# Two layers of graph attention and a routed MLP on one core: routing steps laid between the tiles' statistics

## The reference, cut to what matters

```
x = x + attention(layernorm(x), adj)     # masked softmax over the 64 nodes of a graph
x = x + moe(layernorm(x))                # 8 experts, the two with the largest probability

logits = x_norm @ Wr + br                # 8 per token
top two of softmax(logits)               # ties: the lower expert number first
layer 0: weights p1/(p1+p2), p2/(p1+p2);  layer 1: weights p1, p2
y = w1 * expert[i1](x) + w2 * expert[i2](x)
```

## Time and profile before

| | us |
|---|---|
| median of three runs | 943.96 |
| the three runs | 937.42, 943.96, 946.27 |
| profiled execution, its own time | 937.9 |
| its span | 936.0 |
| VectorE busy | 723.5 |
| block phase of layer 0, `x1w` starts of blocks 0 and 6 (36.53 and 159.01), 6 steps | 122.48 |
| block phase of layer 1, `x1w` starts of blocks 0 and 6 (492.55 and 630.68), 6 steps | 138.13 |

### The profile page before, as it was taken

The page is one execution under the profiler, slowest core; times in us unless marked ns, Lnnn a source line. Parts: engine busy times, 40 slices in busy tenths (PEclk is TensorE's granted clock), DMA queues, the critical chain, the costliest instruction groups (busy, mean ns, idle before and its releaser), DMA issues.

```text
span 936.0 us, 24539 instructions
## 1 busy us (share of the span) xinstructions
PE 711.8 (76%) x6599; PEld 563.6 (60%) x6600; DVE 723.5 (77%) x2663; ACT 491.9 (53%) x1113; POOL 546.9 (58%) x544
## 2 busy tenths in 40 slices
PE   3888877567999999999988887886277877777500
PEld 2666555363899999999556765765236765555400
DVE  6788889762799999999388899997517777787538
ACT  2455665410677777777136566565306655555234
POOL 0037777776277667767400567777764777777720
PEclk9977978857999999999999699798589999999855
DMA  8394333331233323324534454332333333333757
GB/s 228 94 189 116 106 99 95 96 106 61 70 91 87 87 81 85 87 81 136 165 112 125 137 145 150 91 91 74 99 92 100 100 105 99 96 102 99 240 226 321
DMA packets 129399, 111.47 MB, mean 119 GB/s; under 512 B 30306, under 2 KB 112681, under 8 KB 129352
## 3 DMA queue, kind: packets, MB, share of 16 engines
q1 hardware_dynamic: 112072, 77.04, 29.9%
q0 software_dynamic: 17280, 33.87, 11.0%
HBM read 60.32 MB, written 52.36 MB: 120 GB/s over the span
## 4 chain that ended last, share of the span: by engine, by line
PE 35%; DVE 25%; issue 19%; POOL 12%; DMA 5%; ACT 2%; SPq 1%; POOLq 1%; DVEq 0%; ACTq 0%
PE bank L631 10%; PE bank L645 10%; POOL row_buf L457 6%; POOL y_buf L465 6%; PE bank L520 3%; DVE xin L973 3%; DVE stat L912 3%; PE bank L569 2%; PE bank L617 2%; PE bank L517 2%; PE bank L501 2%; DVE x1w L1009 2%; DVE x1w L1013 2%; PE bank L687 1%; DMA xin<-x_buf 1%
## 5 line engine op out<-in xcount | busy, mean ns | idle before, releaser
L457 POOL DMA_INDIRECT row_buf<-pay,slot x256 | 253.4, 990 | 217.8 <-DVE slot L1079 139.7
L465 POOL DMA_INDIRECT y_buf<-g_y,g_dst x284 | 293.3, 1033 | 132.1 <-issue 87.1
L806 ACT ACTIVATE g_xT<-bank 128x512 f16<-128x512 f16 x142 | 84.7, 597 | 171.9 <-PE bank L617 169.0
L631 PE MATMUL bank<-g_xT,w 128*128 128x256 f16 x1278 | 165.8, 276 | 1.5 <-ACT g_xT L806 1.4
L569 PE MATMUL bank<-cst,tri 128*128 128x512 bf16 x518 | 120.2, 388 | 24.9 <-DVE w L1189 14.0
L631 PEld LDWEIGHTS bank<-g_xT,w 128*128 x1278 | 117.6, 99 | 18.6 <-issue 2.1
L569 PEld LDWEIGHTS bank<-cst,tri 128*128 128x128 bf16 x518 | 51.4, 100 | 83.9 <-issue 29.3
L645 PE MATMUL bank<-w,g_h 128*128 x1260 | 84.4, 219 | 17.7 <-DVE g_y L1234 17.7
L813 ACT ACTIVATE xn<-bank,b_cols 128x256 f32<-128x256 f32 x216 | 86.7, 474 | 20.2 <-PE bank L631 11.9
L813 ACT ACTIVATE xt<-bank,b_cols 128x256 f32<-128x256 f32 x210 | 84.4, 475 | 14.0 <-PE bank L631 10.7
L645 PEld LDWEIGHTS bank<-w,g_h 128*128 128x128 f16 x1260 | 76.1, 98 | 25.6 <-issue 23.1
(11 more groups left out here) (191 smaller groups left out, 1312.9 us busy)
## 6 DMA issues: line engine op xcount, KB each, us to landing
g_in<-row_buf SPq DMA_DIRECT2D x142, 130.0 KB, 2.2
yin<-y_buf SPq DMA_DIRECT2D x20, 512.0 KB, 5.7
x_buf<-x1w SPq DMA_DIRECT2D x16, 520.0 KB, 5.4
xin<-x_buf SPq DMA_DIRECT2D x10, 520.0 KB, 5.3
y_buf<-g_y,g_dst POOLq DMA_INDIRECT x284
xin<-in_x_dram SPq DMA_DIRECT2D x8, 512.0 KB, 5.2
adj_in<-in_adj_dram SPq DMA_DIRECT2D x16, 256.0 KB, 3.4
row_buf<-pay,slot POOLq DMA_INDIRECT x256, 2.3
```

The lines of the kernel that those rows point to most:

```text
L457: pool.indirect_dma_start(row_buf[L][:, :], bass.IndirectOffsetOnAxis(ap=slot[q][:, k, t:t + 1], axis=0), pay[q][:, t, :], None).then_inc( ...
L465: pool.indirect_dma_start(y_buf[L][:, :], bass.IndirectOffsetOnAxis(ap=g_dst[k][:, t:t + 1], axis=0), g_y[k][:, t, :], None, bounds_check= ...
L631: last = nc.tensor.matmul(dst, w[:, bass.ds(e * (2 * HID[L]) + (wp * HID[L] + c * P), P)], g_xT[q][:, xp, :], start=(m == 0), stop=(m == 2))
L806: nc.scalar.activation(g_xT[q][:, :, :], x_ps[q], ACT.Copy).then_inc(s.gT_sb, 1)
```

## The change

`statistics` gets a flag `braid`. With it a `pause()` stands behind each of the first seven `bn_stats` too. It is set for the first statistics (`statistics_of`), in both layers, and not for those in `add_attention`. The three empty yields of layer 1 become one. And in `route`, for the first expert alone, `rx` is made ahead and compared with nought and multiplied by the expert numbers in one operation, where there was a comparison, a multiplication and a separate subtraction.

```
+WAIT_LOGITS = 1
...
-            def statistics(src, rstd, nmr, beside, std=None, both=None):
+            def statistics(src, rstd, nmr, beside, std=None, both=None, braid=False):
...
                 for t in range(TILES):
                     last = V.bn_stats(stat[:, t, :], src[:, t, :])
+                    if braid and t < TILES - 1:
+                        pause()
...
                 if L == 1:
-                    for _ in range(3):
+                    for _ in range(WAIT_LOGITS):
                         yield
                     dve.wait_ge(s.lg_copied, n + 1)
...
-                    ch.did(V.tensor_tensor(eq[:, :, :], val[:, :, :], bc(vmax), ALU.is_equal))
-                    yield
-                    ch.did(V.tensor_tensor(cand[:, :, :], eq[:, :, :], rev, ALU.mult))
-                    yield
+                    if k == 0:
+                        ch.did(V.tensor_tensor(rx[:, :, 0:NE], lg[:, :, :], bc(l_max[:, :]), ALU.subtract))
+                        yield
+                        ch.did(V.scalar_tensor_tensor(cand[:, :, :], rx[:, :, 0:NE], 0.0, rev, ALU.is_equal, ALU.mult))
+                        yield
+                    else:
...
                     if k == 0:
-                        V.tensor_tensor(rx[:, :, 0:NE], lg[:, :, :], bc(l_max[:, :]), ALU.subtract)
                         ch.did(V.scalar_tensor_tensor(lg2[:, :, :], hot[:, 0, :, :], -BIG, lg[:, :, :], ALU.mult, ALU.add))
...
-                        statistics(xin[q][:, :, X_AT:X_END], rstd1, nmr1, beside, std=std1[q] if L == 0 else None).then_inc(s.st1, 1)
+                        statistics(xin[q][:, :, X_AT:X_END], rstd1, nmr1, beside, std=std1[q] if L == 0 else None, braid=True).then_inc(s.st1, 1)
```

More of the change, by code:

```diff
@@ L1038, in route @@
                     yield
-                    ch.did(V.tensor_tensor(eq[:, :, :], val[:, :, :], bc(vmax), ALU.is_equal))
-                    yield
-                    ch.did(V.tensor_tensor(cand[:, :, :], eq[:, :, :], rev, ALU.mult))
-                    yield
+                    if k == 0:
[4 more added lines that the diff above has]
+                    else:
+                        ch.did(V.tensor_tensor(eq[:, :, :], val[:, :, :], bc(vmax), ALU.is_equal))
+                        yield
+                        ch.did(V.tensor_tensor(cand[:, :, :], eq[:, :, :], rev, ALU.mult))
+                        yield
                     ch.did(V.tensor_reduce(cmax, cand[:, :, :], AX_X, ALU.max))
```

## The result

The changed kernel takes 946.36 us in the median of 22 runs, the kernel before 940.43 in 22 runs (its first three, which stand ahead, had 943.96). The ratio is 1.0066 with a 95% interval of 1.0049 to 1.0084: 6.2 us slower, where 4.5 were forecast.

What follows compares the result with a forecast made beforehand. No single engine bounds it, but hand-overs, with VectorE's work from `scores` to `x1w` on the path. 1.75 - 0.13 + 1.56 + 1.3 = +4.5 us on 943.96 gives 948.5 us, range 936 to 958.

Steps and rivals of the forecast that it cites:

- D: The prediction's own forecast, 945 to 953 us with the trivial waits and one slow step more or less; chance 0.50.
- The price of a wait: On VectorE, a wait after a small operation adds 0.12 us; a `bn_stats` with its routing step takes 0.45 us.
- rival C: Added waits cost nothing, only layer 1's stalls on the logits stay: +1.3 us, 945.3 us; chance 0.10.
- The pauses that find nothing outstanding: 28 pauses in the first statistics of a layer: between nothing and 3.4 us, taken as nothing.
- Layer 0: Steps 1 to 6: 17 waits for 13, +0.48 us, one operation less, -0.13: net +0.35 us a step.
- The path in layer 0: `slot` 4 passes five delayed steps to GpSimd, +1.75 us; GpSimd's unbroken work then hides step 6.
- The logits: Layer 1: VectorE stalls on ScalarE's logits copy in low-clock steps 5 and 2, +1.56 and +1.3 us.
- Rival A: Layer 1: each stall makes the next step slow, so steps 1 to 6 all stall: +12.1 us, 956 us; chance 0.18.
- Rival B: Layer 1: later `st1` cuts TensorE's idle time, its clock gains, stalls vanish: 943.6 us, or 939.4; chance 0.22.
- The group phase: Same instructions, so its length should not change by more than a us, else the prediction is wrong.

Runs made afterwards that it cites:

- e6: The changed kernel with the wait put ahead of the routing step, behind the next `bn_stats`, in both layers, and five empty yields: 934.39 us, 0.9909 of before.
- e2: The changed kernel with steps laid between statistics in layer 0 alone, logits awaited where they were, fused comparison in both layers: 941.80 us, 1.0012 of before.
- e4: The kernel before with the fused comparison alone, no steps between statistics, logits awaited where they were: 938.02 us, 0.9967 of before.
- e12: e4 timed again, beside e11 on one chip: 940.59 us, 1.0008 of before.
- e3: The changed kernel with steps laid between statistics in layer 1 alone, with the early wait for the logits: 944.43 us, 1.0042 of before.
- e1: The changed kernel again, no edit, for a second profile: 946.73 us, 1.0061 of before.
- e7: e2 with the wait put ahead of the routing step in layer 0: 938.11 us, 0.9973 of before.
- e5: The changed kernel with eight empty yields instead of one, so layer 1 awaits the logits late but keeps its pauses: 942.58 us, 1.0007 of before.
- e8: e4 with `low_parts` in four operations of 256 elements instead of one of 1024: 941.21 us, 0.9986 of before.
- e9: e6 with seven empty yields instead of five, so the logits are awaited later: 938.43 us, 0.9971 of before.
- e10: e6 with one empty yield, as in the change: 937.03 us, 0.9959 of before.
- e11: e6 timed again: 936.15 us, 0.9949 of before.

## Why the prediction was right, step by step

**The forecast time** of 948.5 us came 2.1 us from the 946.36 measured with some luck: the three runs it started from had a median 3.5 us over that of the 22, and the sum of the terms was 1.4 to 1.7 us short. Nor does D's own span of 945 to 953 us follow from its terms, which give 948.5 - 2.1 = 946.4 to 948.5 + 3.4 + 2.1 = 954.0. What follows goes by the differences.

**The price of a wait: right.** 0.45 us a pair, 0.12 of it the wait, and e6 shows that it is the completion, and not the wait's own instructions: with 0.195 us of other work between, pairs are 0.33 apart. The rule of the Trainium skill ("VectorE: DVE Perf Modes", "The DRAIN you can't avoid"), that a semaphore costs nothing extra, doesn't hold for operations of 64 elements here, and rival C with it. Its advice to have fewer operations does: the saved one was worth its 0.13. The pauses that find nothing outstanding cost nothing, as I took them: eight `bn_stats` with such pauses take the same 1.64 us.

**Layer 0: right.** +0.32 us a step in the stretch for +0.35. By timing the waits cost 2.4 us (e2 against e4 and e12) for 5 x 0.48 = 2.4. That the two agree to the tenth is luck, with intervals of 2.5 us; the later start of the groups says 2.9.

**The path in layer 0: only in outline.** I let `slot` 4 carry the delay to GpSimd, which was then to run through at 20.25 us a block. In the profile after, `slot` 4 came at 144.73 us, before the change at 144.79: a step that was slow before was quick there, and it hid the waits. Nor did GpSimd wait for `slot` 4: it worked without a break from block 2 on, and took 21.5 and 21.6 us for blocks 3 and 4 instead of 20.25, for scatters that were held. The groups began 3.9 us later all the same. So the delay did not reach the end of the phase by the one `slot` that I named. What the profile has instead is a `slot` 2 that came 1.2 us later (104.56 us against 103.36) and more held scatters behind it; that these two make up the delay is not shown.

**The logits: right in mechanism, place and price, short in number.** The term was +1.56 and +1.3, 2.9 us in all; e3 against e4 and e12 measures 5.2. The price of a stalled step is the one forecast. Steps at a clock of 0.71 to 0.73 take 23.2 to 23.6 us without the early wait and 24.8 to 25.2 with it, 1.6 more. Steps at 0.64 to 0.66 take 24.1 to 24.6 and 25.3 to 25.7, some 1.2 more: there the wait for ScalarE, 0.31 us in the earlier trace rows, is gone in the stalled steps, as I had it. What was mis-sized is the number of such steps. I counted the two of one profile; there were three in the profiles after and of e3, and two in that of e1. Layer 1's six steps took 142.2 us in the mean of these three profiles and 137.6 in that of the five whose layer 1 is that of before or has the fused comparison alone (before, e2, e4, e7, e12). Of these 4.6 us, eight stalled steps in three profiles make 3.9, and the rest goes with there being 2.7 slow steps a profile and not 2.2.

**Rival A** (every step stalls) did not come. With the early wait 3 (after), 2 (e1) and 3 (e3) of the six steps were under a clock of 0.8; without it 2 (before), 2 (e2), 3 (e4), 2 (e12), 1 (e5), 2 (e7) and 2 (e8). With the waits covered in both layers there was one in each of four profiles (e6, e9, e10, e11), and it stalled. Whether a stall makes a later step slow stays open; these counts don't show it.

**Rival B** (a later `st1` helps TensorE's clock) is not borne out for the change: its mean granted clock was 0.859 and 0.870 in the two profiles, 0.876 before. e5, with the same late `st1`, had 0.886 and five quick steps in one profile, but took 942.58 us in the median.

**The group phase** is the same work but not the same length. From the first transpose of layer 0's groups to the first `x1w` of layer 1 it took 255.0 us before, 256.7 after, 255.0 in e1 and 256.9 in e4. By the bound of one us I set, the profile after would have failed, and the same kernel in e1 passed: the bound was too narrow for single profiles.

## What to carry to other kernels

Laying one chain's steps into another's saves time only where two steps then share one wait, or where a wait has foreign work between it and the operation it waits for. `operation A; step B; wait for B` pays the whole completion of B, and adding more such pairs adds more waits; `operation A; wait for the last B; step B` hides it behind A, if A is long enough: 0.195 us was, for a wait of 0.12. And before a routing step is pulled forward on an in-order engine, look when its input arrives in the slowest steps, not in the mean one: everything behind it inherits the stall.

## What the runs showed of the hardware that was not expected

A scatter that GpSimd starts while VectorE runs `low_parts` (1024 elements, two inputs in SBUF) ends 2.05 us after `low_parts` began, whenever it began itself. In the profile after: started 0.39 us in, at 158.26, it took 1.66. Before, 0.12 us in (`low_parts` at 606.49):

```profile
606.61 1.93 POOL L457 DMA_INDIRECT row_buf<-pay,slot  x1 [0.30 <-issue]
```

606.61 + 1.93 - 606.49 = 2.05. So it is in the 13 profiles in which `low_parts` is one operation: 147 scatters that started 0.03 to 1.08 us into it ended 2.04 to 2.07 us after its start. One that started before it, or at most 0.02 us in, was not held (`low_parts` at 137.41, before):

```profile
137.43 0.96 POOL L457 DMA_INDIRECT row_buf<-pay,slot  x1 [0.30 <-issue]
```

A free scatter takes 0.96, so a held one ends as if it were served from 1.09 us after the start of `low_parts` on, just before VectorE starts its next operation at 1.14. The Trainium skill ("SBUF — State Buffer", section "Who interferes with whom") has it that a VectorE instruction with two SBUF inputs contends with a GpSimd instruction that reads SBUF. The trace agrees if a scatter's issue counts as such a read, which the page doesn't say; the same section also has an observation the other way, of a `tensor_tensor` that did not stall a DMA. e8's pieces bring the hold down to some 0.2 us. Whether it costs the kernel time is open, as said at e8.

Two timings of one kernel on different chips, each beside its own runs of before, came out 4 permille apart twice (e4 and e12, e6 and e11), and their intervals only just overlap. Differences of 2 us between versions need more than one such timing.
